# Three projections that end without waiting for their last stores, and operand loads in 12 transfers a unit in place of 24

## What is computed

```
x_n = (x - mean) * rsqrt(var + 1e-5) * ln_gamma + ln_beta
q, k, v = split(x_n @ W_qkv + b_qkv)          # 16 heads of 8 features
scores = q @ k^T * 8 ** -0.5                  # 1024 x 1024 for each head and batch
attn = softmax(scores)
x = x + (attn @ v) @ W_proj + b_proj
```

## Time and profile before

| | us |
|---|---|
| median of 3 runs | 3560.78 |
| lowest and highest run | 3556.45, 3560.81 |
| the profiled execution | 3568.88 |
| its span, first to last instruction | 3567.1 |
| TensorE, VectorE, ScalarE, GpSimd busy | 2992.9 (84%), 2607.5 (73%), 2145.6 (60%), 486.4 (14%) |
| mean granted TensorE clock, share of full speed | 0.923 |

### The profile page before, as it was taken

One profiled execution on the slowest core, in us unless ns is written; L12 is line 12 of the kernel. 1 busy time (PEld: TensorE's weight loads), 2 busy tenths in 40 slices (PEclk: granted clock), 3 DMA queues, 4 the chain that ended last, 5 costly groups with the idle time before them and its releaser, 6 DMA issues. The chain is left out here.

```text
span 3567.1 us, 51582 instructions
## 1 busy us (share of the span) xinstructions
PE 2992.9 (84%) x18320; PEld 1209.2 (34%) x18320; DVE 2607.5 (73%) x6022; ACT 2145.6 (60%) x2739; POOL 486.4 (14%) x753
## 2 busy tenths in 40 slices
PE   5999997896999999985999898947569988889836
PEld 2333333443122222214455555535412222222214
DVE  6999973666999999946666666631868888888821
ACT  2566673223377777773555455512479989999812
POOL 2000001333000000004000000013221011102023
PEclk7899998997799999997999999968779999999958
DMA  5442202333211111000000000012362223221112
GB/s 146 62 108 57 33 13 49 66 78 113 28 27 27 23 22 22 12 5 31 1 1 1 7 1 7 1 62 65 104 124 31 31 33 39 31 29 20 53 28 70
DMA packets 172978, 148.30 MB, mean 42 GB/s; under 512 B 79672, under 2 KB 130632, under 8 KB 172720
## 3 DMA queue, kind: packets, MB, share of 16 engines
q1 hardware_dynamic: 168624, 137.21, 19.5%
q0 software_dynamic: 4096, 7.78, 0.7%
HBM read 95.13 MB, written 49.68 MB: 41 GB/s over the span
## 5 line engine op out<-in xcount | busy, mean ns | idle before, releaser
L1324 ACT ACTIVATE a_probs<-a_scores 128x1024 f32<-128x1024 f32 (+3 forms) x896 | 791.4, 932 | 372.2 <-PE a_scores L1206 235.1
L1347 DVE TENSOR_REDUCE a_part_max<-a_slot_ps 128x1 f32<-128x512 f32 x1280 | 798.5, 683 | 32.7 <-PE a_slot_ps L1184 31.2
L2219 DVE TENSOR_TENSOR a_probs<-a_logit_ps,a_gate 128x1024 f32<-128x1024 f32 x512 | 602.3, 1219 | 102.6 <-ACT a_gate L2078 99.3
L1184 PE MATMUL a_slot_ps<-a_k_op,a_q_op 48*128 48x512 bf16 (+3 forms) x1792 | 579.8, 380 | 90.0 <-PEq L123 28.1
L2083 ACT ACTIVATE a_probs<-a_probs 128x2048 f32<-128x2048 f32 x256 | 488.0, 1906 | 8.5 <-DVE a_probs L2219 4.3
L1206 PE MATMUL a_scores<-a_q_op,a_k_op 51*128 51x512 bf16 (+3 forms) x1792 | 453.3, 362 | 7.1 <-ACT a_probs L1324 6.1
L1226 PE MATMUL a_o_ps<-a_probs,a_v_op 128*32 128x512 f32 (+3 forms) x3584 | 438.6, 561 | 1.2 <-ACT a_o_sb L1311 0.6
L1184 PEld LDWEIGHTS a_slot_ps<-a_k_op,a_q_op 48*128 48x128 bf16 x1792 | 150.2, 94 | 692.5 <-DVE a_part_max L1347 469.4
L1984 PE MATMUL a_logit_ps<-space 96*128 96x512 bf16 x1024 | 303.8, 387 | 73.6 <-DVE a_probs L2219 62.8
L2078 ACT ACTIVATE a_gate<-a_diff_ps 128x1024 f32<-128x1024 f32 x256 | 261.3, 1021 | 59.3 <-PE a_diff_ps L1984 51.3
L1997 PE MATMUL a_o_ps<-a_probs,a_v_op 128*32 128x512 f32 x2048 | 275.7, 610 | 7.0 <-DVE a_o_sb L2212 3.1
(11 more groups left out here) (401 smaller groups left out, 3928.0 us busy)
## 6 DMA issues: line engine op xcount, KB each, us to landing
e_coef<-coef_dram SPq DMA_DIRECT2D x16, 1024.0 KB, 10.1
a_q_op<-scratch_q SPq DMA_DIRECT2D x384, 32.0 KB
a_k_op<-scratch_k SPq DMA_DIRECT2D x384, 32.0 KB
scratch_q<-p_parts SPq DMA_DIRECT2D x24, 384.0 KB, 3.3
scratch_k<-p_parts SPq DMA_DIRECT2D x24, 384.0 KB, 3.5
space<-scratch_k SPq DMA_DIRECT2D x192, 32.0 KB
space<-scratch_g SPq DMA_DIRECT2D x192, 32.0 KB
space<-scratch_q SPq DMA_DIRECT2D x192, 32.0 KB
```

The lines of the kernel that those rows point to most:

```text
L1184: nc.tensor.matmul(out[:, 0:width], q_op[g][r0:r0 + MAX_ROW, e, qt * P:(qt + 1) * P], k_op[g][r0:r0 + MAX_ROW, e, kh * CH:kh * CH + width] ...
L1324: nc.scalar.activation(probs[gs % NB][:, 2 * e:2 * e + 2, off:CH], scores[e][:, :, off:CH], ACT.Exp, scale=scale).then_inc(probs_done, 1)
L1347: nc.vector.tensor_reduce(part_max[u % 2][:, kh, col:col + 1], slot[:, 0:w], axis=AX.X, op=ALU.max).then_inc(slot_done, 1)
L2219: nc.vector.tensor_tensor(probs[gs % 4][:, m, :, :], logit_ps[m][:], gate[gs % 2][:], op) \
```

## The change

It has three parts.

1. A class `Stores` holds the `stored` and `v_stored` semaphores and the buffers that the last chunks use (`late`: 4 of 8 part buffers and 2 of 4 value buffers in p0 and p1, 3 of 6 and 1 of 2 in p3), allocated outside the projection so that the attention block doesn't take their SBUF. The projection ends with a wait for the other buffers alone (chunks 4 and 5 in p0 and p1, chunk 6 in p3). The wait for the late ones stands in the attention: in a0 and a1 before the operands of unit 4, in a3 before the operands of batch 1.
2. `load_qk` issues 12 transfers. `PAIR_PARTS` is reordered so that pairs with the same part of q follow each other, and a run of 3, 2 or 1 pairs is one transfer for each operand and half, of 24, 16 or 8 partitions and 4 KB each. For q the same 8 rows are read count times. The columns of the weights are permuted on the host (`by_rows_of_heads`), so that the two 2 KB rows of a partition are neighbours in DRAM. Four transfers each follow the stores of chunks 3, 4 and 5.
3. In p3 the values of the first unit are loaded behind the stores of chunk 3 (the wait for the first batch takes in the value stores), no longer at the start of a3.

```diff
+class Stores:
+    def __init__(self, nc, ctx, name, items, ring, late, v_shape, v_ring, v_late):
+        self.stored = [nc.alloc_semaphore(f"{name}_stored{i}") for i in range(ring)]
+        self.v_stored = [nc.alloc_semaphore(f"{name}_v_stored{i}") for i in range(v_ring)]
+        self.early, self.v_early = ring - late, v_ring - v_late
+        self.parts = [ctx.enter_context(nc.sbuf_tensor(f"{name}_late_parts{i}", [P, 3, CH], BF16)) for i in range(late)]
+        self.values = [ctx.enter_context(nc.sbuf_tensor(f"{name}_late_values{i}", v_shape, FP32)) for i in range(v_late)]
+        self.items, self.last, self.v_last = items, 16 * (CHUNKS * items // ring), 16 * (CHUNKS // v_ring)
+    def wait_all_but_last(self, sp):
+        for i in range(self.early):
+            sp.wait_ge(self.stored[i], self.last)
+        for i in range(self.v_early):
+            sp.wait_ge(self.v_stored[i], self.v_last)
...
                 if c == 3:
-                    for i in range(4):
-                        sp.wait_ge(stored[i], 16)
+                    stores.wait_first_batch(sp)
                 if c >= 3:
                     load_early(sp, c)
...
-            for i in range(2 * NB):
-                sp.wait_ge(stored[i], 16 * (CHUNKS * ITEMS // (2 * NB)))
-            for i in range(4):
-                sp.wait_ge(v_stored[i], 16 * (CHUNKS // 4))
+            stores.wait_all_but_last(sp)
...
-PAIR_PARTS = [(0, 0), (0, 1), (1, 0), (0, 2), (2, 0), (1, 1)]
+PAIR_PARTS = [(0, 0), (0, 1), (0, 2), (1, 0), (1, 1), (2, 0)]
+PAIR_RUNS = ((0, 0, 3), (1, 3, 2), (2, 5, 1))
...
-        for n in parts:
-            qp, kp = PAIR_PARTS[n]
+        for qp, first, count in list(PAIR_RUNS)[parts.start:parts.stop]:
             for half in range(2):
-                r0 = half * HALF_ROWS + n * 8
-                for op, dram, part in ((self.q, self.qs, qp), (self.k, self.ks, kp)):
-                    src = dram[b, part, g * 32:(g + 1) * 32, :].rearrange("(e h r) t -> h r e t", e=2, h=2)
-                    sp.dma_start(op[g][r0:r0 + 8, :, :], src[half, :, :, :]).then_inc(self.qk_loaded[g], 16)
+                r0, f0 = half * HALF_ROWS + first * 8, g * 32 + half * 16
+                rows = self.ks[b, 0:count, f0:f0 + 16, :].rearrange("n (r e) t -> n r (e t)", e=2)
+                sp.dma_start(self.k[g][r0:r0 + count * 8, :, :].rearrange("p e t -> p (e t)"), rows).then_inc(self.qk_loaded[g], 16)
+                rows = self.qs[b, qp:qp + 1, f0:f0 + 16, :].rearrange("n (r e) t -> n r (e t)", e=2).to_broadcast([count, 8, 2 * T])
+                sp.dma_start(self.q[g][r0:r0 + count * 8, :, :].rearrange("p e t -> p (e t)"), rows).then_inc(self.qk_loaded[g], 16)
...
@@ narrow_attention
                 if u + 1 < UNITS:
                     load_max(u + 1)
+                if u == 0:
+                    stores.wait_last(sp)
...
@@ project_cosine
                 if c == 3:
-                    for i in range(RING):
-                        sp.wait_ge(stored[i], 16)
+                    stores.wait_first_batch(sp)
+                    operands.load_v(sp, 0, 0)
...
@@ cosine_attention
-            operands.load_v(sp, 0, 0)
             for g in range(1, GROUPS):
```

More of the change, by code:

```diff
@@ L114, in apply_norm, with wait_first_batch, wait_last, project @@
     return ins
-def project(nc, name, src, mv, rstd, wq, wk, wv, qs, ks, vs, ident, load_early, gain=None, qk_bias=None, v_bias=None, fresh=None):
+class Stores:
[6 more added lines that the diff above has]
+        self.items, self.last, self.v_last = items, 16 * (CHUNKS * items // ring), 16 * (CHUNKS // v_ring)
+    def wait_first_batch(self, sp):
+        for i in range(2 * self.items):
+            sp.wait_ge(self.stored[i], 16)
+        for i in range(2):
+            sp.wait_ge(self.v_stored[i], 16)
+    def wait_all_but_last(self, sp):
[3 more added lines that the diff above has]
+            sp.wait_ge(self.v_stored[i], self.v_last)
+    def wait_last(self, sp):
+        for i in range(self.early, len(self.stored)):
+            sp.wait_ge(self.stored[i], self.last)
+        for i in range(self.v_early, len(self.v_stored)):
+            sp.wait_ge(self.v_stored[i], self.v_last)
+def project(nc, name, src, mv, rstd, wq, wk, wv, qs, ks, vs, ident, load_early, stores, gain=None, qk_bias=None, v_bias=None, fresh=None):
     NB, ITEMS = 4, 2
@@ L137, in project @@
         rem = [sb(f"rem{i}", [P, CH]) for i in range(NB)]
-        parts = [sb(f"parts{i}", [P, 3, CH], BF16) for i in range(2 * NB)]
-        v_sb = [sb(f"v_sb{i}", [P, CH]) for i in range(4)]
+        parts = [sb(f"parts{i}", [P, 3, CH], BF16) for i in range(NB)] + stores.parts
+        v_sb = [sb(f"v_sb{i}", [P, CH]) for i in range(2)] + stores.values
         stats, eps, std, trial = sb("stats", [P, TILES * 6]), sb("eps", [P, 1]), sb("std", [P, TILES]), sb("trial", [P, TILES])
@@ L148, in project @@
         stats_done, mv_done, std_done, root_step = (sem(n) for n in ("stats_done", "mv_done", "std_done", "root_step"))
-        stored = [sem(f"stored{i}") for i in range(2 * NB)]
-        v_stored = [sem(f"v_stored{i}") for i in range(4)]
+        stored, v_stored = stores.stored, stores.v_stored
         n_loads = 3 + sum(a is not None for a in (gain, qk_bias, v_bias))
@@ L1084, in load_early, with narrow_attention @@
                 sp.dma_start(tile[:], self.consts[n]).then_inc(self.masks_loaded, 16)
-        self.load_qk(sp, 0, range(2 * (c - 3), min(2 * (c - 2), len(PAIR_PARTS))))
-def narrow_attention(nc, name, shape, operands, scale, ctx_nat, consts, floor=None, fills=None, soft=None):
+        self.load_qk(sp, 0, range(c - 3, min(c - 2, len(PAIR_RUNS))))
+def narrow_attention(nc, name, shape, operands, scale, ctx_nat, consts, stores, floor=None, fills=None, soft=None):
     H, S, BANKS = 4, shape.n, 3
@@ L1494, in project_cosine @@
         rem = [sb(f"rem{i}", [P, CH]) for i in range(RING)]
-        parts = [sb(f"parts{i}", [P, 3, CH], BF16) for i in range(RING)]
-        vpad = [sb(f"vpad{i}", [P, CPT, 8, 32]) for i in range(2)]
+        parts = [sb(f"parts{i}", [P, 3, CH], BF16) for i in range(ITEMS)] + stores.parts
+        vpad = [sb("vpad0", [P, CPT, 8, 32])] + stores.values
         x_ps, v_ps = ps("x_ps"), ps("v_ps")
@@ L1503, in project_cosine @@
              "unit_done", "unitT_ready", "hi_done", "rem_done", "mid_done", "lo_done", "v_ready", "v_done", "v_preset"))
-        stored = [sem(f"stored{i}") for i in range(RING)]
-        v_stored = [sem(f"v_stored{i}") for i in range(2)]
+        stored, v_stored = stores.stored, stores.v_stored
         block = ctx.enter_context(nc.Block())
@@ L3131, in four_layers @@
                     fills = ZeroFills(nc, only_here, slots, results)
[L3132 removed]
+                    with ExitStack() as flying:
+                        stores = Stores(nc, flying, "p0", 2, 8, 4, [P, CH], 4, 2)
+                        project(nc, "p0", x, mv, rstd, a["L0_Wq"], a["L0_Wk"], a["L0_Wv"], scratch[0], scratch[1], scratch_v, ident,
+                                operands.load_early, stores, fresh=fresh)
+                        narrow_attention(nc, "a0", shape, operands, shape.hd ** -0.5, nat, consts, stores, fills=fills, soft=soft)
                     soft_layer(nc, "e0", x, nat, xn1, mv, rstd, soft, coef_dram, fills.filled, descending[16], ident)
```

35 lines of the change are left out of this document (17 added, 18 removed).

## The result

| | us |
|---|---|
| median after, 14 runs | 3549.72 (3543.25 to 3556.66) |
| median before, 14 runs | 3563.43 (3556.45 to 3571.25) |
| ratio, with its 95% interval | 0.9962 (0.9954 to 0.9970) |
| profiled execution after, its span | 3550.24, 3548.4 |

The change saves 13.5 us (10.7 to 16.4); 13.0 were forecast.

A forecast was written before the change was run, and what follows sets the result against it. TensorE is busy 84% of the span, so only the ends of p0, p1 and p3 can pay: -2.7 - 2.9 - 7.4 = -13.0 us, from a median of 3560.78 to 3547.8, range 3540 to 3555.5.

The forecast's parts named there:

- What bounds: Whole kernel: transfer changes pay only at the ends of p0, p1 and p3; a0's unit stays at 28.5 us.
- p3, -7.4: End of p3: without the last stores' wait and with early values, a3's first gate comes at 2608.8, not 2616.16.
- Number of engines: Operand loads: the outermost count of 3 or 2 sets how many DMA engines work, not the 24 or 16 partitions.
- p0, -2.7, and p1, -2.9: Ends of p0 and p1: attention starts earlier by these us, once chunk 5's stores land behind loads on engine 0.
- The sum, -13.0: Whole kernel: the gains at p0, p1 and p3 together, in us.
- SyncE's issuing, "4.2 us" fewer: p0 and p1: twelve fewer transfers at 0.35 us an issue save SyncE 4.2 us; 2.1 of it counts in p0.
- rival of wide loads: Partitions set the engines, so p0 gains 5.0, p1 7.1, p3 7.4: -19.5 us, 3541.3; chance 0.27.
- rival held by the queue: SyncE leaves p0 and p1 no earlier, so only p3 pays: -7.4 us, 3553.4; chance 0.20.
- slower rival: Engine 0 bounds p0, p1 and a0: at 0.35 us a row, +33 us, 3594; chance 0.04.

The follow-up runs named there:

- values_late: The changed kernel with only p3's first values loaded at the start of a3 again, as before; timed once, 3551.3 us.
- flat_source: The changed kernel with each load reading 24 or 16 neighbouring rows of one part, so its products are not the layer's; timed once, 3542.4 us.
- last_stores_later: The changed kernel with the last stores (chunks 6 and 7, in p3 chunk 7) issued first thing in the attention; ratio 0.9970 to the kernel before.
- stores_only: The changed kernel with the old 24 operand transfers of 8 partitions, keeping the dropped waits and p3's early values; ratio 0.9963 to the kernel before.
- rows_outermost: The changed kernel with the 8 rows as outermost dimension of each grouped load and the pairs second; ratio 0.9956 to the kernel before.
- loads_only: The changed kernel with the old waits for all stores and p3's values at a3's start, keeping the 12 transfers; ratio 1.0021 to the kernel before.
- by_eights: The changed kernel with operands in 24 transfers of 8 partitions again, each partition one row of 4 KB; ratio 0.9955 to the kernel before.

## Why the prediction was right

- **What bounds:** right. The gain lies at the three ends, and a0's unit stays at 28.5 us.
- **p3, -7.4:** 7.6 at the gate, which the prediction counts (12.1 and 12.5 us behind GpSimd's last subtraction before, 4.7 and 4.8 after), by the mechanism named; the first gate comes 1.88 us after SyncE's last issue, 1.91 were forecast. That the values had to come early with the wait is shown by values_late. The prediction took the operands' landing as past; in the first profile it was 0.2 us behind the start.
- **Number of engines:** right by the ones' row and against partitions. Share 0.14 to 0.18 in after, 0.44 with 8 rows outermost, 0.70 with 24. The rule that the prediction cited from the Trainium skill ("DMA: Bandwidth & Descriptors", section "Why a DMA increments its semaphore by 16 and not by 1"), the largest number up to 16 that divides the slowest dimension on both sides, gives 3 and 2 for after, 8, and 12 for 24 plain rows; by the shares the runs agree (flat_source: 0.70 of 16 is 11.2).
- **p0, -2.7, and p1, -2.9:** 1.8 and 2.4 measured. The mechanism (chunk 5's stores behind 64 rows on engine 0) is shown by last_stores_later. The starts come 20.25 and 19.7 us behind the first early issue, where the prediction's times give 19.0 and 19.3. Two terms were too small, by the packets in the trace of after: the first row of 4 KB starts 1.85 us (p0) and 1.57 us (p1) behind the first early issue, where 1.0 was taken, and a row takes 0.182 and 0.189 us in the mean, where 0.175 was taken. With 6.0 for two chunks' stores and 64 rows they put the landing of chunk 5's stores 19.5 and 19.7 us behind the first early issue. If the start follows a landing as it follows an issue in stores_only, by 0.65 us, these stores had landed in last_stores_later at 19.4 in p0 and 18.6 in p1. So p0 comes out, and in p1 the sum is 1.1 us too long, which stays open. In p0 the profiles of before lie 0.8 apart, so p0's own gain is known no better than that.
- **The sum, -13.0:** 13.5 measured (10.7 to 16.4), and 11.9 at the three ends. That the whole came within 0.5 us of the forecast is partly luck: p0 and p1 gave 1.4 us less than forecast, p3 0.3 more, and the remaining 1.6 us stands at none of the three ends.
- **SyncE's issuing, "4.2 us" fewer:** wrong, and it carried no part of the sum only because engine 0 was taken as the bound. Four grouped issues fill 3.2 us (45.14 to 48.31), eight of the old ones 2.8. The rival of wide loads rested on this saving (-5.0 and -7.1). rows_outermost, with 8 engines and the same long issues, brought 4.0 and 4.05; flat_source, with 11 engines and short issues, 6.0 and 5.7. So wide loads would have been worth about what the rival said, but not from a source in groups, which is what the change reads.
- **The rival held by the queue:** in part. SyncE's last issue does end where it ended before (19.3 and 18.7 us behind the first early issue, before 18.3 to 19.1 and 18.8), with issues stretched to 1.8 us. What the rival left out is that the wait behind it shrinks all the same.
- **The slower rival:** did not come in the change, a row cost 0.18 to 0.19 us and not 0.276. But its place was real: with the old waits kept, the same loads cost 7.5 us (loads_only).

## What to carry to other kernels

A wait for stores at the end of a stage cost their landing on the busiest DMA engine, 3.4 us here and 7.1 where narrow loads crowded it. What takes the place of the wait is the next thing in the same queues: at p3 the values' load (4.6 us of the gain), then the issue of the stores, then the landing of the last operand load. Fewer and larger transfers need save nothing: count the engines that a transfer keeps and the time that its issue takes, since half as many loads of 3 groups were a loss of 7.5 us when made alone. Buffers that outlive the stage allow their stores to be issued in the next one. That paid only once nothing else bound: with eight engines for each load it took 4 us from each of p0 and p1 (18.1 to 14.0), with the narrow loads next to nothing (20.25 to 20.1, 19.7 to 19.2).

## What the hardware showed that was not expected

- Where nothing stretched it, an issue on SyncE took 0.27 to 0.30 us for a load of 8 neighbouring partitions, 0.31 to 0.45 for 24 partitions from one run of rows, 0.60 for 8 partitions that lie 3 apart, and 0.65 to 0.9 for 24 partitions from a source in groups.
- In windows where loads flow alone, eight engines that load 8 neighbouring partitions together moved about 8 GB/s each, in rows of 2 KB (70 GB/s at 0.57) as of 4 KB (by_eights, 74 at 0.57); eight engines that write 3 partitions each moved 20 (rows_outermost, 143 at 0.44), and three engines 26 (after, 74 at 0.18). Whether the neighbours in SBUF or those in the source are the reason was not settled.
